# A product with V that waits for its transposed scores batch by batch instead of once

## The reference

```
xn = layernorm(x)                                   # x: 4 x 2048 x 2048, f32
# retention ("ret"), 16 heads of 128
q, k = xpos(xn @ wq), xpos(xn @ wk);  v = xn @ wv
scores = (q @ k.T) * 128**-0.5 * decay_mask         # causal, gamma**(t-s)
y = scores @ v
s = (silu(xn @ w_g) * groupnorm(y)) @ w_proj
# ffn branch: one of three per token, by argmax(xn @ w_router.T)
out0 = xn + bias;  out1 = xn + xn @ w_down.T @ w_up.T
h = xn + softmax_attention(layernorm(xn)) @ wo.T    # causal, 16 heads of 128
out2 = h + gelu(layernorm(h) @ w_ff1.T) @ w_ff2.T
x = x + s * silu(where(route == 0, out0, where(route == 1, out1, out2)))
```

## Time and profile before

| | us |
|---|---|
| three runs | 5884.43, 6013.81, 6110.53 |
| their median | 6013.81 |
| the profiled execution | 5886.67 |
| its span (slowest core, 7) | 5885.1 |
| spans of the eight cores | 5835.2 to 5885.1 |
| mean granted TensorE clock of the cores | 0.803 to 0.812 |

### The profile page before, as it was taken

The page is one execution under the profiler, slowest core; times in us unless marked ns, Lnnn a source line. Parts: engine busy times, 40 slices in busy tenths (PEclk is TensorE's granted clock), DMA queues, the critical chain, the costliest instruction groups (busy, mean ns, idle before and its releaser), DMA issues.

```text
span 5885.1 us, 63395 instructions; the slowest of 8 cores (5835.2 to 5885.1 us)
## 1 busy us (share of the span) xinstructions
PE 3808.0 (65%) x18468; PEld 1761.6 (30%) x18468; DVE 1638.5 (28%) x3980; ACT 904.0 (15%) x1869; POOL 372.2 (6%) x330
## 2 busy tenths in 40 slices
PE   1276666667676677546655655665556489969496
PEld 1223333333333222223223322332222134423232
DVE  5703323333323213732222222222220400002122
ACT  2101111111111132111222122212210011100000
POOL 0000000000000000100000000000000011111010
PEclk9998787878787788767766776777668799989698
DMA  3113222323131144603422432242414334466665
GB/s 105 69 21 47 32 39 29 42 27 44 24 47 24 20 54 50 83 21 52 73 42 42 65 59 42 45 74 47 70 32 62 57 95 113 110 158 149 179 145 138
DMA packets 396791, 386.31 MB, mean 66 GB/s; under 512 B 309152, under 2 KB 333984, under 8 KB 389312
## 3 DMA queue, kind: packets, MB, share of 16 engines
q0 software_dynamic: 336960, 268.72, 29.9%
q1 hardware_dynamic: 59520, 113.54, 5.9%
HBM read 508.31 MB, written 109.05 MB: 105 GB/s over the span
## 4 chain that ended last, share of the span: by engine, by line
PE 54%; DVE 19%; issue 11%; DMA 9%; ACT 7%; DVEq 1%; ACTq 0%; SPq 0%; POOLq 0%; POOL 0%
PE pbA L842 5%; PE pbB L842 4%; DMA wff<-ff2T_bf 4%; PE pbB L783 4%; PE pbA L783 4%; PE pbA L1670 3%; PE pbB L1670 3%; PE pbA L1810 3%; ACT scp L1013 3%; PE pbA L724 3%; PE pbA L988 2%; PE pbY L1090 2%; PE pbS L1090 2%; PE pbT L1059 2%; DVE scT_sb L1071 2%
## 5 line engine op out<-in xcount | busy, mean ns | idle before, releaser
L842 PE MATMUL pbA<-xn_allT,wvh 128*128 128x512 bf16 x1024 | 293.6, 452 | 37.6 <-DVE vtok L868 13.6
L1810 PE MATMUL pbA<-xn_allT,wff 128*128 128x512 bf16 x1024 | 236.5, 394 | 105.7 <-DMA xn_allT<-hg_sp 77.9
L1090 PE MATMUL pbY<-vtok,scT_sb 128*128 128x128 bf16 x1024 | 122.4, 294 | 280.1 <-DVE scT_sb L1074 280.1
L842 PE MATMUL pbB<-xn_allT,wvh 128*128 128x512 bf16 x1024 | 261.6, 414 | 52.6 <-DVE vtok L868 40.2
L1670 PE MATMUL pbA<-bufA,wqh 128*128 128x512 bf16 x1024 | 234.2, 382 | 78.2 <-DVE bufA L1633 68.2
L1090 PE MATMUL pbS<-vtok,scT_sb 128*128 128x128 bf16 x1280 | 119.9, 256 | 235.5 <-DVE scT_sb L1074 235.5
L1059 PE MATMUL pbT<-eye_sb,scp 128*128 128x128 bf16 x2304 | 265.8, 290 | 0.6
L868 DVE COPY vtok<-pbT 128x512 bf16<-128x512 bf16 x128 | 54.3, 424 | 725.6 <-PE pbT L860 725.6
L1810 PE MATMUL pbB<-xn_allT,wff 128*128 128x512 bf16 x1024 | 225.3, 381 | 15.3 <-DMA wff<-ff2T_bf 15.3
L1059 PEld LDWEIGHTS pbT<-eye_sb,scp 128*128 128x128 bf16 x2304 | 217.1, 133 | 59.3 <-issue 58.9
L783 PE MATMUL pbB<-xn_allT,wkh 128*128 128x512 bf16 x1024 | 233.1, 381 | 2.5 <-DVE kb_sb L799 2.5
(11 more groups left out here) (287 smaller groups left out, 5258.4 us busy)
## 6 DMA issues: line engine op xcount, KB each, us to landing
wff<-ff2T_bf POOLq DMA_DIRECT2D x32, 2048.0 KB, 15.2
ff1T_bf<-ff1T POOLq DMA_DIRECT2D x8, 4096.0 KB, 25.2
ff2T_bf<-ff2T POOLq DMA_DIRECT2D x8, 4096.0 KB, 25.8
wqh<-ff1T_bf POOLq DMA_DIRECT2D x64, 512.0 KB, 5.9
p0x<-x_all SPq DMA_DIRECT2D x16, 1024.0 KB, 4.8
xn_allT<-hg_sp SPq DMA_DIRECT2D x2, 8192.0 KB, 37.8
p0x<-x_own SPq DMA_DIRECT2D x8, 1024.0 KB, 4.8
wqh<-w_qkv POOLq DMA_DIRECT2D x16, 512.0 KB, 8.2
```

The source lines that it names most:

```text
L842: inst = t.matmul(pb[key][:, 0:cw], self.wv_h[buf][:, ct, :], self.xn_allT[:, ct, c0:c0 + cw], start=(ct == 0), stop=(ct == CT - 1))
L1090: inst = t.matmul(pb[ykey][:, 0:P], self.scT_sb[:, st * P:(st + 1) * P], self.vtok[:, st * P:(st + 1) * P], start=(st == 0), stop=(st == n ...
L1810: inst = t.matmul(pb[key][:, 0:cw], wff2[buf][:, ft, :], hg3[:, ft, 0:cw], start=(ft == 0), stop=(ft == FT - 1))
```

## The change

In `stage_consume` the token of each batch's evacuation is collected in a list. The y group waits first for `v_done` and the bank, and then, ahead of its blocks 0 and 8, for the batch that holds the next eight blocks. Before, it waited ahead of everything for the last batch, and after that for `v_done` and the bank. Transposes, evacuations, matmuls and increments are the same; row tiles with at most 8 blocks (0 to 3) keep one wait for the evacuation, the others have two.

```diff
                 scp = self.sc_pair[rt % 2]
+                ev_batch = []
                 for g0 in range(0, nst, 8):
...
                     self.V(_)
                     self.bfree[tkey] = [self.tok(s_v)]
+                    ev_batch.append(self.tok(s_v))
                 scT_tok = self.tok(s_v)
...
-                def _(t, rt=rt, nst=nst, scT_tok=scT_tok, ykey=ykey):
-                    self.wt(t, scT_tok, v_done, *self.bfree[ykey])
+                def _(t, rt=rt, nst=nst, ev_batch=ev_batch, ykey=ykey):
+                    self.wt(t, v_done, *self.bfree[ykey])
                     for st in range(nst):
+                        if st % 8 == 0:
+                            self.wt(t, ev_batch[st // 8])
                         inst = t.matmul(pb[ykey][:, 0:P],
                                         self.scT_sb[:, st * P:(st + 1) * P],
                                         self.vtok[:, st * P:(st + 1) * P],
```

## The result

The changed kernel takes 5780.2 us (median of 9 runs), the kernel before 5886.45 (10 runs, those shown above among them). In some runs of either kernel the cores of one die or both had a lower clock and took longer, so all ratios and gains here leave those runs out, and the rows of the changed kernel, in whose profiled execution cores 4 to 7 were such a die, are those of core 1 (the median span of cores 0 to 3 is 5755.1 us). The ratio is 0.9803, with a 95% interval of 0.979 to 0.9816: 116 us less. The forecast was 5783.4 us, 103 us less and a ratio of 0.982. It is the 116 us that compare with the 103, and not the median 5780.2 with 5783.4.

A forecast was written before the change was run, and what follows sets the result against it. It took a ring of engines waiting on each other, not plain TensorE work, as the bound. Wait order 54.3 us plus split 49.0 us made 103.3 us, from 5886.7 to 5783.4 us; 8-in-10 range 5735 to 5920.

The forecast's parts named there:

- Part one: Ahead of each y group, two satisfied waits no longer follow the releasing one: 0.212 us in 256 groups, 54.3 us.
- Part two: In row tiles 4 to 7 the first eight y matmuls start on batch 0's release: 1.53 us a pass, 49.0 us.
- the 0.91 us between tile 7's batches: Time between the ends of tile 7's two VectorE batches, the most its y start could move; 0.44 or 0.83 us counted.
- a microsecond taken from the start of y is a microsecond of the end: In the attention tile loops, time saved ahead of y shortens the kernel equally, unless something else holds the next step.
- The idle time ahead of y: L1090's waits for VectorE were to fall from 516 us to about 394.
- What was costed at nothing: Extra wait in 128 groups, at most 13.6 us, and writing scT_sb while TensorE reads it, at most 49 us: taken as 0.
- The waits ahead of the scores: Satisfied waits TensorE's queue works off after y, limiting the split: tiles 4 and 5 keep 0.17 us at the high clock.
- rivals 1 and 3: Clock levels: 1, high level comes earlier, 5751 us, chance 0.18; 3, low level catches more V chunks, 5889 us, 0.05.
- the 0.01 that I had named: Prediction wrong if the attentions' granted clock moves by more than 0.01 from 0.78 and 0.72.
- the drift allowed each way: Clock drift of 13.6 us either way, in the forecast's own range of 5765 to 5805 us.
- Rival 2: Only one part, wait order or split, pays: 5838 or 5832 us, chance 0.12.
- the ring: Second-attention loop: y, TensorE's scores, ScalarE's exponentials, VectorE's row sum, next batch 0; in the first attention scores, transposes, VectorE.

The follow-up runs named there:

- two more waits: Kernel before with two more long-satisfied v_done waits behind the three ahead of the y matmuls: 5950.9 us, ratio 1.0117.
- seven waits elsewhere: Changed kernel with seven of the eight waits for the last y of each tile left out ahead of each v chunk: 5629.4 us, ratio 0.9579.
- the order alone: Kernel before with v_done and the bank waited for first and the last batch's evacuation last, still one wait for all of scT_sb: 5817.5 us, ratio 0.9888.
- without repeated waits: No engine waits again for a semaphore value already waited for: changed kernel 5357.2 us, ratio 0.9114; kernel before 5416.8 us, ratio 0.9217.
- tile 7 with the order: Changed kernel with the new wait order but the split only in row tile 7; tiles 4 to 6 wait for the last batch: ratio 0.9809.
- one wait more: Kernel before with one more satisfied wait behind the three ahead of the y matmuls: 5936.8 us, one execution, no interval.
- the split alone: Changed kernel with batch 0's wait put back ahead of v_done and the bank, and batch 1's wait ahead of block 8: ratio 0.990.

## Why the prediction was right

**Part one, the order of the waits.** Right in its mechanism to the hundredth: 0.33 us became 0.12 in every one of the 256 groups, two more waits made it 0.54, and seven waits elsewhere cost 0.73. The trace and the runs put a wait at 0.104 to 0.106 us. The 50 to 100 ns that the Trainium skill gives for a sequencer's read of a semaphore ("Advanced Engine Details and Errata", Network/Comms) are thus a little less than what a whole wait instruction costs TensorE's queue here. As a term of the sum, 54.3 us compare with 66 (51 to 80) measured alone.

**Part two, the split.** Right where it can be seen: y starts on the copy, and tile 7 has a gap in its weight loads, 0.20 us in the first attention and 0.14 in the second. Tiles 4 and 5 have none; tile 6 has one of 0.07 us in the first attention. As a term, 49.0 us compare with the 50 that lie between the order alone and the whole change, and with 60 without repeated waits; the 56 forecast with its own order effect compare with 59 (31 to 87) measured alone. One reading was not typical: the 0.91 us between tile 7's batches is 0.66 in the median pass of the first attention. It changed nothing, since only 0.44 of it counted at the high level.

What failed is the way from the tiles to the pass. Tiles 4 to 6 were to bring 30 of the 49 us and bring some 11; tile 7 with the order brought 112 instead of 73. The tiles saved what they should (1.07 and 1.98 us a pass), and the passes became 0.2 and 3.35 us shorter. The step of the prediction that failed is thus "a microsecond taken from the start of y is a microsecond of the end": it took the clock levels of the rest of the pass as given.

**The idle time ahead of y.** 516 to 402 us; the forecast was 394. That is 114 us less waiting, and the kernel became 116 faster. The two need not agree so well: gaps inside the y groups, some 6 us in all, stand beside the 402, and the clock's moves are in the 116 alone.

**What was costed at nothing.** The extra wait instruction inside the group is hidden: ten matmuls take 1.22 us with and without it. VectorE writes one part of scT_sb while TensorE reads another, and both keep their durations (the copy 0.69 us, the masked piece 0.28; over all of them the means are 529 and 282 ns in both kernels). The waits ahead of the scores took a part of the split in the first attention, about what the forecast had them take, and not the whole of it.

**The clock (rivals 1 and 3).** Both happen, at the same time and in different places, which I had weighed as alternatives. In the changed kernel the first attention's tile loop became 4.0 us a pass shorter where 3.2 was the sum, while its v stretch became 0.4 and q 0.3 longer. The sum had also left the share of y matmuls at the high level at 21% (bank Y) and 61% (bank S). By the means of 273 and 271 ns in the rows of the changed kernel it is 43% and 45%. Windows of the changed kernel, core 1, to be read beside those of before and of the order alone:

```profile
1000.00:1900.00 900.00, 631.66 (x3292) 291.40 (x3292) 300.54 (x697) 113.53 (x201) 48.07 (x61) 0.82 0.27 34
2700.00:4200.00 1500.00, 958.50 (x4845) 471.05 (x4843) 362.27 (x1031) 327.95 (x839) 52.19 (x53) 0.72 0.40 56
```

0.81 to 0.82 and 0.73 to 0.72, within the 0.01 that I had named. So the clock's gains and losses nearly cancelled for the change as a whole, and the sum came within 13 us, less than the drift allowed each way. With the order alone they did not cancel (0.83 and 0.69). The parts add up to 66 + 59 = 125 us against 116 together, which the intervals allow. That the sum of 103 us came so close to 116 is thus partly luck: a single part of it was off by 39 us.

**Rival 2** (one part pays nothing) is refuted for the whole kernel by the two runs of one part each, though the order alone did pay nearly nothing in the second attention. **Rival 4** (something else holds the ring) is refuted.

## What to carry to other kernels

A wait that is long satisfied is not free when it stands behind the one that releases: put the wait that ends last at the end, and drop waits that an earlier one of the same engine already covers. In this kernel a helper that remembers what each engine has waited for is worth four times the change studied, in a few lines: on the kernel before 461 us (ratio 0.9217) and on the changed one 405, against 116. Splitting a wait by batches pays as far as the early work covers the late batch and the queue has time for the waits of what follows, and the extra wait costs nothing if enough is queued ahead of it. And when an idle time is put down to another engine by the profile, compare it with that engine's end: here 0.12 us after it was a release, 0.3 or 0.8 a queue of waits.

## What the hardware did that was not expected

A few tenths of a microsecond taken out of every tile moved the clock level in parts of the pass that no edit touched: mean granted clock 0.69, 0.72 and 0.73 in the second attention for kernels that differ only in waits. The lengths of its passes seem to gather at certain values: medians of 116.05, 115.99, 112.62, 119.48 and 109.23 us before, with the order alone, with the change, with two waits more and with fewer ahead of v. These lie 3.4 us apart. Yet one wait more gave 118.28, with most passes from 116.5 to 119.8, the split alone 113.48, and the kernel before without repeated waits 105.04. So no run had to fall on such a value. Whether they mean anything, and why they are these, I leave open; no run here varied the clock by itself. For forecasts it means that a sum of small savings in such a kernel holds roughly over all passes and not for a part of them: the measured changes were 12% above the sum for the whole change, 5% for the split alone, 22% for the order alone, 27% for two waits more, and 53% for the order with the split of tile 7.
